# Neighbourhood attention: each head on 32 rows of its own, the scores of two heads issued as a pair

## The chip, the cores and the metric

The program runs on one core of a Trainium2 chip. The time is the device time of one execution in microseconds, the median of the runs shown. TensorE is PE in the profile (PEld are its weight loads), VectorE is DVE, ScalarE is ACT, GpSimd is POOL.

## The reference

Two transformer layers over 64 images of 96 x 96, each cut into 36 patches and a class token (37 tokens of 192 numbers). Layer 0 is a patch embedding, a linear attention with 4 heads of 64 and a soft mixture of 64 experts. Layer 1 is a block with neighbourhood attention and a routed mixture of 8 experts. The change lies in the neighbourhood attention, which sees the 64 x 37 tokens as an image and has 4 heads of 24:

```python
qkv = xs @ qkv_w.T + qkv_b
qkv = qkv.reshape(H, W, 3, nh, dh).transpose(2, 3, 0, 1, 4)
q, kmat, vmat = (qkv[0], qkv[1], qkv[2])
q = q * dh ** (-0.5)
...
logits = jnp.einsum('nhwd,nhawbd->nhwab', q, kk)
...
logits = logits + bias
attn = jax.nn.softmax(logits.reshape(nh, H, W, k * k), axis=-1).reshape(nh, H, W, k, k)
out = jnp.einsum('nhwab,nhawbd->nhwd', attn, vv)
out = out.transpose(1, 2, 0, 3).reshape(H, W, D)
return out @ proj_w.T + proj_b
```

Each query looks at a window of 5 x 5 positions (`k = 5`), clipped at the borders. All is computed in 32-bit floats.

## The kernel before

The 64 rows of 37 tokens are cut into 22 tiles of three rows, 111 tokens each (`TP`). A tile's windows lie in seven rows, so its scores are 111 x 259 (`KW`) per head, with the positions outside the window masked by an added bias.

The stage has two parts. In the first, over pairs of tiles, two small products and a GELU give `xg`, the input in 96 rows by tokens; `keys` multiplies it by `wk` into `kT`. In the second, a pipeline over the tiles, every engine has a list of steps, each with a lag: in turn s a step with lag g works on tile s - g. TensorE's list in each turn is: `query` (lag 0), `values` (3), `scores` of heads 0 and 1 (1), `proj` (5), `scores` of heads 2 and 3 (1), `transpose_w` (3), `fc2` (5), `values_out` (4). VectorE's is: copy of transposed weights (4), `reciprocal` (2), `logits` (1), value copy (3), `spread` (0), `residual` (5). ScalarE does the exponentials (1) and copies, GpSimd multiplies the exponentials by the reciprocal sums (2).

`over_tiles` writes the first 8 turns out straight, then a register loop with four turns per pass, then the last turns straight. In the second part the loop covers turns 8 to 19, on every engine. Engines work strictly in the order of their lists; between them stand semaphores only.

The four heads lie side by side in the 96 rows of `kT`. To keep heads apart, `spread` (L1269) copies the query four times: copy n holds head n's 24 rows and zeros elsewhere (a product with the table `head`). Each of the four score products (L1432) thus contracts over all 96 rows. Heads 0 and 2 write PSUM bank 1, heads 1 and 3 bank 2. A score product waits (`s_nl`) until the head two before it has been emptied from its bank, which is one instruction per head in `logits` (L1296): it adds the bias, writes the scores to SBUF and takes the row maximum. After four heads the maxima are negated (L1298) and ScalarE starts on the exponentials (L1331).

The transposes are L1442 and L1443, the projection L1465, the values in four column strips L1458. In layer 0, L753 is a score product of heads in two halves of 64 rows, in two banks; L738 comes behind it.

## Time and profile before

| | |
|---|---|
| median of 3 runs | 1119.67 us (1112.85 to 1121.09) |
| profiled execution | 1121.94 us, span 1120.0 us |
| TensorE busy | 951.7 us, 85% |
| VectorE busy | 528.6 us, 47% |
| ScalarE busy | 323.8 us, 29% |
| GpSimd busy | 312.6 us, 28% |
| mean granted clock of TensorE | 0.84 |
| first part of the stage | about 580 to 632 us |
| second part of the stage | about 635 to 770 us |

Busy shares are means over stages with different limits. The chain of waits goes back from the last instruction to whatever released it, and so names the engine that sets the pace in each stretch. The timeline lists instructions in order; a bracket behind one says how long its engine was idle before it and who ended that. The end of a product is modelled and includes its way through the array, so records of neighbouring products overlap.

### The profile page before, as it was taken

To read this page: it belongs to the slowest core of one execution; us is meant where nothing else is said; L and a number is where in the kernel's file an instruction comes from. 1 tells how busy PE (TensorE), PEld (TensorE's weight loads), DVE (VectorE), ACT (ScalarE), POOL (GpSimd) and SP (SyncE) were. 2 spreads that over 40 slices of the span, in tenths; PEclk is the share of its full clock that TensorE was granted. 3 is DMA by queue.
4 is the path that set the end of the run, shared out by engine and by line. 5 is a ranking of instruction groups with operands and counts; after the bars stand their busy time and mean duration, and the time that the engine had idled before them with its cause. 6 is when DMAs were issued, how large, how long until landed. Compare 5 with 4: busy or idle time off the path is not lost.

```text
span 1120.0 us, 18357 instructions
## 1 busy us (share of the span) xinstructions
PE 951.7 (85%) x5804; PEld 664.2 (59%) x5804; DVE 528.6 (47%) x1712; ACT 323.8 (29%) x908; POOL 312.6 (28%) x308
## 2 busy tenths in 40 slices
PE   6667999968999998887769899996575999999990
PEld 5555777746664555554545467774563777777670
DVE  5983678864443232222753368864672222222210
ACT  1332233323343322222122256662201222222210
POOL 3881000000000000000042045541017277677444
PEclk9995899975557999999975579996556999999995
DMA  8778000000002999995350000000205244544222
GB/s 253 218 271 346 1 0 0 0 1 1 1 1 80 419 423 422 422 424 215 104 141 1 0 1 2 0 2 8 60 3 140 53 83 82 83 80 74 35 22 21
DMA packets 64187, 125.82 MB, mean 112 GB/s; under 512 B 26910, under 2 KB 47184, under 8 KB 54912
## 3 DMA queue, kind: packets, MB, share of 16 engines
q1 hardware_dynamic: 34176, 115.69, 28.8%
q0 software_dynamic: 29952, 9.36, 6.4%
q8 instruction: 34, 0.56, 0.2%
q14 instruction: 25, 0.20, 0.1%
HBM read 112.83 MB, written 11.98 MB: 111 GB/s over the span
## 4 chain that ended last, share of the span: by engine, by line
PE 67%; DMA 12%; DVE 9%; issue 6%; POOL 2%; ACT 2%; SPq 1%; DVEq 0%; POOLq 0%; ACTq 0%
PE bank L1747 14%; DMA ys<-eo 10%; PE bank L1757 6%; PE bank L738 4%; PE bank L743 3%; PE bank L1432 3%; PE bank L909 2%; PE bank L1518 2%; PE bank L1048 2%; PE bank L927 2%; PE bank L1442 2%; PE bank L1458 2%; PE bank L774 1%; PE bank L907 1%; PE bank L925 1%
## 5 line engine op out<-in xcount | busy, mean ns | idle before, releaser
L1747 PE MATMUL bank<-zT,w 96*128 96x372 f32 x512 | 161.8, 477 | 0.0
L1156 POOL MEMSET xg<- 96x74 f32 x1 | 0.2, 157 | 478.0 <-PE bank L1130 478.0
L1747 PEld LDWEIGHTS bank<-zT,w 96*128 96x128 f32 x512 | 97.4, 191 | 61.0 <-issue 0.5
L1692 POOL DMA_INDIRECT out_dram<-yr,put x48 | 105.7, 2203 | 90.0 <-issue 62.0
L1803 DVE TENSOR_TENSOR hT<-sg,bank 128x372 f32<-128x372 f32 x64 | 34.7, 542 | 126.4 <-PE bank L1747 126.4
L1678 POOL DMA_INDIRECT zr<-z_rows,take x48 | 66.5, 1385 | 85.4 <-issue 83.9
L990 DVE COPY eh<-bank 128x384 f32<-128x384 f32 x32 | 17.8, 558 | 119.4 <-PE bank L1026 119.4
L1048 PE MATMUL bank<-w2s,eg 128*64 128x192 f32 x768 | 69.4, 330 | 0.0
L1776 ACT ACTIVATE sg<-bank 128x372 f32<-128x372 f32 x64 | 30.7, 480 | 128.0 <-PE bank L1747 128.0
L715 PE MATMUL bank<-wtok_g,xT 128*111 128x192 f32 x264 | 47.9, 332 | 20.9 <-DVE y L628 20.9
L1757 PE MATMUL bank<-w2r,hT 128*124 128x192 f32 x384 | 63.7, 326 | 0.0
L1757 PEld LDWEIGHTS bank<-w2r,hT 128*124 128x124 f32 x384 | 62.2, 187 | 0.2
L1022 PE MATMUL bank<-w1s,xy 128*64 128x384 f32 x256 | 49.7, 510 | 12.4 <-DMA w1s<-in_w_dram 11.8
L1048 PEld LDWEIGHTS bank<-w2s,eg 128*64 128x64 f32 x768 | 52.5, 137 | 11.3 <-issue 5.4
L1195 POOL TENSOR_TENSOR nl<-nl,nr 111x1036 f32<-111x1036 f32 x22 | 42.1, 1912 | 61.1 <-DVE nr L1305 61.1
L1331 ACT ACTIVATE nl<-nl,nn 111x259 f32<-111x259 f32 x88 | 43.8, 500 | 48.4 <-DVE nn L1298 48.4
L715 PEld LDWEIGHTS bank<-wtok_g,xT 128*111 128x111 f32 x264 | 41.8, 176 | 26.8 <-DVE y L628 15.3
L1432 PE MATMUL bank<-kT,qx 96*111 (+1 forms) x176 | 53.1, 432 | 1.3 <-DVE nm L1296 1.3
L738 PE MATMUL bank<-hnT,cb 96*128 96x111 f32 x352 | 49.8, 300 | 0.0
L738 PEld LDWEIGHTS bank<-hnT,cb 96*128 96x128 f32 x352 | 45.9, 210 | 2.4 <-issue 0.4
L1296 DVE CUSTOM_DVE_ANT_0 nl<-bank,bias 111x259 f32<-111x259 f32 x88 | 36.7, 424 | 15.2 <-issue 14.7
L743 PE MATMUL bank<-cb,hnT 96*111 96x448 f32 x88 | 41.3, 596 | 0.0
(277 smaller groups left out, 1801.0 us busy)
## 6 DMA issues: line engine op xcount, KB each, us to landing
w1s<-in_w_dram SPq DMA_DIRECT2D x32, 1152.0 KB, 12.6
w2s<-in_w_dram SPq DMA_DIRECT2D x32, 1152.0 KB, 14.7
xt<-in_x_dram SPq DMA_DIRECT2D x22, 336.0 KB, 3.9
xT<-in_xT_dram SPq DMA_DIRECT2D x22, 333.0 KB, 3.6
w<-in_w_dram SPq DMA_DIRECT2D x8, 768.0 KB
ys<-eo SPq DMA_DIRECT2D x64, 48.0 KB, 9.3
w2r<-in_w2r_dram SPq DMA_DIRECT2D x8, 384.0 KB
e<-ys SPq DMA_DIRECT2D x21, 96.0 KB, 2.0
```

The costliest lines, as they stand in the source:

```text
L715: last = nc.tensor.matmul(bank[2 + q % 2][0:TP, 0:ED], xT[q][:, k, :], wtok_g[:, k, :], start=(k == 0), stop=(k == KC - 1))
L738: last = nc.tensor.matmul(bank[1][:, j * TP:(j + 1) * TP], wqk[:, c, j * 128:(j + 1) * 128], hnT[b][:, c, :], start=(c == 0), stop=(c == 1))
L743: last = nc.tensor.matmul(bank[2][0:TP, 0:VGW], hnT[b][:, c, :], wvg[:, c, :], start=(c == 0), stop=(c == 1))
L1022: nc.tensor.matmul(bank[2 * b + part][e * B:(e + 1) * B, 0:HALF_HID], xy[:, 0, p + e * NPAIR, :], w1s[q][:, cols], start=True, stop=False)
L1048: last = nc.tensor.matmul(bank[6 + b][e * B:(e + 1) * B, 0:ED], eg[b][:, j, e, :], w2s[q][:, e, j, :], start=(j == 0), stop=(j == HB - 1))
L1195: nc.gpsimd.tensor_tensor(nl[q][:], nl[q][:], nr[b][:].unsqueeze(2).to_broadcast([TP, NHN, KW]), ALU.mult).then_inc(s_nw, 1)
L1331: last = nc.scalar.activation(nl[q][:, head, :], nl[q][:, head, :], ACT.Exp, bias=nn[b][:, head:head + 1], accum_out=nsum[b][:, head:head ...
L1432: nc.tensor.matmul(bank[1 + head % 2][0:TP, 0:KW], qx[q % 2][:, head, :], kT[:, bass.ds(first, KW)], start=True, stop=True).then_inc(s_nS, 1)
L1678: nc.gpsimd.indirect_dma_start(zr[b][:, j, :], None, z_rows, bass.IndirectOffsetOnAxis(ap=take[:, k:k + 1], axis=0), bounds_check=NROW - 1 ...
L1692: nc.gpsimd.indirect_dma_start(rows_out, bass.IndirectOffsetOnAxis(ap=put[:, k:k + 1], axis=0), yr[e % 2][:, j, :], None, bounds_check=OUT ...
L1747: last = nc.tensor.matmul(bank[2 + 2 * (m % 2) + part][:, 0:HS], w13[b][:, c, at:at + 128], zT[b][:, c, half * HS:(half + 1) * HS], start= ...
L1757: last = nc.tensor.matmul(bank[6 + j % 2][0:SP_, 0:ED], hT[:, m, j * SP_:(j + 1) * SP_], w2r[b][:, m, :], start=(m == 0), stop=(m == EH // ...
```

## The change

Weights and biases of queries and keys are padded from 96 to 128 columns, so that head n lies in rows 32n to 32n + 23 and zeros follow. `qx` is then one copy of 128 x 111 instead of 96 x 4 x 111, made by a plain add-and-scale. A score product takes its head's 32 rows of `qx` and `kT`. The waits on `s_nl` move ahead of each pair: heads 0 and 1 wait until all four heads of the tile before have been emptied, heads 2 and 3 until heads 0 and 1 have. Ahead of the queries of tiles 0, 1 and 2, six products of `identity` with 256 columns of `kT` are added, whose result nobody reads. TensorE's list is written out straight for all turns (`straight`); the other engines keep their loops.

```diff
--- before.py
+++ after.py
@@ -60,10 +60,10 @@
 PACK_B = [("wqk", HALF, 2 * QKW), ("wvg", HALF, 2 * VGW), ("wo", 128, 2 * ED), ("causal", TP, 2 * TP),
           ("phi", HALF, 2 * NE), ("scale", HALF, 1), ("image", TP, GB + 1), ("b1s", 128, NE * HB)]
 
-PACK_C = [("fc1", HALF, 2 * WN), ("conva", WN, CONV), ("convb", CONV, WN), ("wq", WN, WN), ("wk", WN, WN),
+PACK_C = [("fc1", HALF, 2 * WN), ("conva", WN, CONV), ("convb", CONV, WN), ("wq", WN, 128), ("wk", WN, 128),
           ("wv", WN, WN), ("proj", NHN * VW, WN), ("fc2", WN, ED), ("bv", TP, WN), ("bfc2", TP, ED),
-          ("bfc1", WN, 1), ("bconva", CONV, 1), ("bconvb", WN, 1), ("bq", WN, 1), ("bk", WN, 1), ("bproj", WN, 1),
-          ("head", WN, NHN), ("router", HALF, 2 * EX), ("before", TP, TP), ("count", TP, SP_), ("number", TP, T), ("spare", SP_, NST), ("real", TP, T),
+          ("bfc1", WN, 1), ("bconva", CONV, 1), ("bconvb", WN, 1), ("bq", 128, 1), ("bk", 128, 1), ("bproj", WN, 1),
+          ("router", HALF, 2 * EX), ("before", TP, TP), ("count", TP, SP_), ("number", TP, T), ("spare", SP_, NST), ("real", TP, T),
           ("gain", HALF, 2 * EX)]
 
 
@@ -101,6 +101,13 @@
                 step(i + (u - lag), (u - lag) % unroll)
     for s in range(stop, n + lags):
         turn(s)
+
+
+def straight(stages, n, buffers):
+    for s in range(n + max(lag for lag, _ in stages)):
+        for lag, step in stages:
+            if 0 <= s - lag < n:
+                step(s - lag, (s - lag) % buffers)
 
 
 def tower(nc, ins, rows_out):
@@ -261,7 +268,7 @@
         near = [sb(f"near{v}", [TR, NHN, KW]) for v in range(2)]
         bias = [sb(f"bias{v}", [TP, NHN, KW]) for v in range(4)]
         xg = sb("xg", [WN, XCOLS])
-        kT = sb("kT", [WN, XCOLS])
+        kT = sb("kT", [128, XCOLS])
         hp = [sb(f"hp{b}", [TP, 2, ED]) for b in range(2)]
         hpT = [sb(f"hpT{b}", [HALF, 2, PAIR]) for b in range(2)]
         fx = [sb(f"fx{b}", [WN, PAIR]) for b in range(2)]
@@ -270,7 +277,7 @@
         vsrc = [sb(f"vsrc{b}", [WN, TP]) for b in range(2)]
         vn = [sb(f"vn{q}", [TP, NHN, VW]) for q in range(4)]
         vl = [sb(f"vl{i}", [TP, NHN, VW]) for i in range(3)]
-        qx = [sb(f"qx{b}", [WN, NHN, TP]) for b in range(2)]
+        qx = [sb(f"qx{b}", [128, TP]) for b in range(2)]
         nl = [sb(f"nl{q}", [TP, NHN, KW]) for q in range(4)]
         nm = [sb(f"nm{b}", [TP, NHN]) for b in range(2)]
         nn = [sb(f"nn{b}", [TP, NHN]) for b in range(2)]
@@ -1254,7 +1261,7 @@
 
             def keys(p, b):
                 dve.wait_ge(s_fK, p + 1)
-                nc.vector.tensor_scalar(kT[:, bass.ds(PADR * S + p * PAIR, PAIR)], bank[4][0:WN, 0:PAIR], Cc["bk"], None, ALU.add).then_inc(s_fKc, 1)
+                nc.vector.tensor_scalar(kT[:, bass.ds(PADR * S + p * PAIR, PAIR)], bank[4][:, 0:PAIR], Cc["bk"], None, ALU.add).then_inc(s_fKc, 1)
 
             over_tiles(dve, [(0, normalize), (4, convb), (2, fc1), (5, keys)], T // 2)
 
@@ -1266,7 +1273,7 @@
                     dve.wait_ge(s_fV, t)
                 if after(t, 2):
                     dve.wait_ge(s_nS, 4 * t - 4)
-                nc.vector.scalar_tensor_tensor(out=qx[b][:], in0=bank[0][0:WN, 0:TP].unsqueeze(1).to_broadcast([WN, NHN, TP]), scalar=Cc["bq"], in1=Cc["head"].unsqueeze(2).to_broadcast([WN, NHN, TP]), op0=ALU.add, op1=ALU.mult).then_inc(s_nq, 1)
+                nc.vector.tensor_scalar(qx[b][:], bank[0][:, 0:TP], Cc["bq"], float(np.float32(DN ** -0.5)), ALU.add, ALU.mult).then_inc(s_nq, 1)
 
             def value(j, dst):
                 dve.wait_ge(s_fV, j + 1)
@@ -1392,20 +1399,23 @@
                 pe.wait_ge(s_fg, p + 1)
                 if after(p, 1):
                     pe.wait_ge(s_fKc, p)
-                nc.tensor.matmul(bank[4][0:WN, 0:PAIR], Cc["wk"], xg[:, bass.ds(PADR * S + p * PAIR, PAIR)], start=True, stop=True).then_inc(s_fK, 1)
+                nc.tensor.matmul(bank[4][:, 0:PAIR], Cc["wk"], xg[:, bass.ds(PADR * S + p * PAIR, PAIR)], start=True, stop=True).then_inc(s_fK, 1)
 
             over_tiles(pe, [(3, convb), (0, transpose_h), (1, fc1), (2, conva), (4, keys)], T // 2)
             pe.wait_ge(s_fKc, T // 2)
             pe.wait_ge(s_hTc, 2 * T + T // 2)
 
             def query(t, q):
+                if isinstance(t, int) and t < 3:
+                    for _ in range(6):
+                        nc.tensor.matmul(bank[5][:, 0:256], ident, kT[:, 0:256], start=True, stop=True)
                 if after(t, 1):
                     pe.wait_ge(s_nq, t)
                 if after(t, 4):
                     pe.wait_ge(s_fVc, t - 1)
                 elif t == 0:
                     pe.wait_ge(s_fVc, 2)
-                nc.tensor.matmul(bank[0][0:WN, 0:TP], Cc["wq"], xg[:, bass.ds(PADR * S + t * TP, TP)], start=True, stop=True).then_inc(s_nQ, 1)
+                nc.tensor.matmul(bank[0][:, 0:TP], Cc["wq"], xg[:, bass.ds(PADR * S + t * TP, TP)], start=True, stop=True).then_inc(s_nQ, 1)
 
             def value(j, b):
                 pe.wait_ge(s_fv, j + 1)
@@ -1424,12 +1434,13 @@
                 value(j, j)
 
             def scores(t, q, heads):
-                first = (B - WIN + PADR) * S if isinstance(t, int) and t == T - 1 else t * TP
+                first = (B - WIN + PADR) * S if t == T - 1 else t * TP
                 pe.wait_ge(s_nq, t + 1)
+                if t or heads[0]:
+                    pe.wait_ge(s_nl, 4 * t + heads[0])
                 for head in heads:
-                    if after(t, 1) or head >= 2:
-                        pe.wait_ge(s_nl, 4 * t + head - 1)
-                    nc.tensor.matmul(bank[1 + head % 2][0:TP, 0:KW], qx[q % 2][:, head, :], kT[:, bass.ds(first, KW)], start=True, stop=True).then_inc(s_nS, 1)
+                    rows = slice(head * VW, (head + 1) * VW)
+                    nc.tensor.matmul(bank[1 + head % 2][0:TP, 0:KW], qx[q % 2][rows, :], kT[rows, first:first + KW], start=True, stop=True).then_inc(s_nS, 1)
 
             def transpose_w(t, q):
                 pe.wait_ge(s_nw, t + 1)
@@ -1468,8 +1479,8 @@
                 pe.wait_ge(s_nz, t + 1)
                 nc.tensor.matmul(bank[7][0:TP, 0:ED], nz[q % 2][:], Cc["fc2"], start=True, stop=True).then_inc(s_nF, 1)
 
-            over_tiles(pe, [(0, query), (3, values), (1, lambda t, q: scores(t, q, (0, 1))), (5, proj),
-                            (1, lambda t, q: scores(t, q, (2, 3))), (3, transpose_w), (5, fc2), (4, values_out)], T, unroll=4, tail=2)
+            straight([(0, query), (3, values), (1, lambda t, q: scores(t, q, (0, 1))), (5, proj),
+                      (1, lambda t, q: scores(t, q, (2, 3))), (3, transpose_w), (5, fc2), (4, values_out)], T, 4)
 
 
         def route_act(act):
@@ -1922,14 +1933,14 @@
             for n in range(NHN):
                 near[v // 2, 0:TP, n] = np.where(ok, rpb[n][np.where(ok, dr, 0), np.where(ok, dt, 0)], 0)
     qkv, bqkv = f["L1_attn_qkv_w"], f["L1_attn_qkv_b"]
+    heads = lambda a: np.pad(a.reshape(-1, NHN, DN), ((0, 0), (0, 0), (0, VW - DN))).reshape(-1, NHN * VW)
     cc = pack_rows(PACK_C, {
         "fc1": chunks(f["L1_attn_fc1_w"].T), "conva": f["L1_attn_convA_w"].T, "convb": f["L1_attn_convB_w"].T,
-        "wq": qkv[0:WN].T, "wk": qkv[WN:2 * WN].T, "wv": qkv[2 * WN:].T, 
+        "wq": heads(qkv[0:WN].T), "wk": heads(qkv[WN:2 * WN].T), "wv": qkv[2 * WN:].T, 
         "proj": np.pad(f["L1_attn_proj_w"].T.reshape(NHN, DN, WN), ((0, 0), (0, VW - DN), (0, 0))).reshape(NHN * VW, WN),
         "fc2": f["L1_attn_fc2_w"].T, "bv": rows(bqkv[2 * WN:], TP), "bfc2": rows(f["L1_attn_fc2_b"], TP),
         "bfc1": col(f["L1_attn_fc1_b"]), "bconva": col(f["L1_attn_convA_b"]), "bconvb": col(f["L1_attn_convB_b"]),
-        "bq": col(bqkv[0:WN]), "bk": col(bqkv[WN:2 * WN]), "bproj": col(f["L1_attn_proj_b"]),
-        "head": (np.arange(WN)[:, None] // DN == np.arange(NHN)[None, :]).astype(np.float32) * np.float32(DN ** -0.5),
+        "bq": heads(bqkv[None, 0:WN]).T, "bk": heads(bqkv[None, WN:2 * WN]).T, "bproj": col(f["L1_attn_proj_b"]),
         "router": chunks(f["L1_ffn_gate_w"].T), "before": (w[:, None] < w[None, :]).astype(np.float32),
         "count": np.tile(np.arange(SP_, dtype=np.float32)[None, :], (TP, 1)),
         "spare": 1.0 + B * S + np.arange(SP_)[:, None] + SP_ * (np.arange(NST) % SJ)[None, :],
```

TensorE, the first turns of the second part, before (L1414 value, L1408 query, L1432 scores):

```order
L1414 MATMUL bank<-cc,vsrc 111x96 x2
L1408 MATMUL bank<-xg,cc 96x111 x2
L1432 MATMUL bank<-kT,qx 111x259 x4
L1408 MATMUL bank<-xg,cc 96x111
L1432 MATMUL bank<-kT,qx 111x259 x4
L1408 MATMUL bank<-xg,cc 96x111
```

and the same place in the changed kernel (L1424 value, L1411 the added products, L1418 query, L1443 scores):

```order
L1424 MATMUL bank<-cc,vsrc 111x96 x2
L1411 MATMUL bank<-kT,identity 128x256 x6
L1418 MATMUL bank<-xg,cc 128x111
L1411 MATMUL bank<-kT,identity 128x256 x6
L1418 MATMUL bank<-xg,cc 128x111
L1443 MATMUL bank<-kT,qx 111x259 x4
L1411 MATMUL bank<-kT,identity 128x256 x6
L1418 MATMUL bank<-xg,cc 128x111
```

The order of queries and scores is the same; six wide products stand ahead of each of the first three queries.

TensorE, the start of a loop pass, before:

```order
L98 UNCONDITIONAL_BRANCH
L1405 REGISTER_ALU
L1408 ISA
L1408 MATMUL bank<-xg,cc 96x111
L1414 MATMUL bank<-cc,vsrc 111x96
L1431 ISA
L1432 ISA
L1432 MATMUL bank<-kT,qx 111x259 x2
L1462 REGISTER_ALU
L1464 REGISTER_ALU
L1465 MATMUL bank<-noT,cc 96x111
```

and the same turn in the changed kernel:

```order
L1418 MATMUL bank<-xg,cc 128x111
L1424 MATMUL bank<-cc,vsrc 111x96
L1443 MATMUL bank<-kT,qx 111x259 x2
L1476 MATMUL bank<-noT,cc 96x111
L1443 MATMUL bank<-kT,qx 111x259 x2
```

The products stand in the same order, with the projection between the two pairs of scores; the register and branch instructions are gone.

## Rows read from the trace of the kernel before

**Rows 1.** The page: busy time, share and instructions of each engine.

```profile
PE 951.7 (85%) x5804; PEld 664.2 (59%) x5804; DVE 528.6 (47%) x1712; ACT 323.8 (29%) x908; POOL 312.6 (28%) x308
```

**Rows 2.** Stretches: length, busy (count) of PE, PEld, DVE, ACT, POOL; PEclk, DMA, GB/s.

```profile
580.00:635.00 55.00, 52.35 (x135) 26.03 (x135) 19.21 (x49) 14.44 (x31) 13.06 (x13) 0.50 0.01 4
635.00:656.00 21.00, 17.59 (x53) 11.93 (x54) 9.38 (x48) 7.08 (x26) 4.91 (x5) 0.50 0.00 0
656.00:757.00 101.00, 97.53 (x1021) 75.45 (x1019) 77.51 (x359) 65.43 (x231) 51.21 (x59) 1.00 0.01 1
757.00:857.00 100.00, 57.07 (x314) 50.86 (x315) 59.59 (x191) 14.91 (x39) 20.02 (x17) 0.52 0.21 53
```

**Rows 3.** Chain of waits, 628 to 775: start us, us, what was waited for.

```profile
634.95 0.70 PE bank L1408 x2
...
655.21 0.88 PE bank L1432 x2
...
666.95 1.10 PE bank L1432 x4
...
672.16 1.10 PE bank L1432 x4
...
677.22 1.03 PE bank L1432 x4
...
691.10 0.89 PE bank L1432 x4
692.18 1.03 PE bank L1432 x4
...
732.31 1.03 PE bank L1432 x4
...
746.47 0.47 PE bank L1432 x2
```

**Rows 4.** Timeline of a loop turn: start us, us, engine, line, operation [idle before].

```profile
690.94 1.05 PE L1432 MATMUL bank<-kT,qx 96*111 x4
...
691.60 0.42 DVE L1296 CUSTOM_DVE_ANT_0 nl<-bank,bias 111x259 f32<-111x259 f32 x1 [0.19 <-issue]
...
692.39 0.08 DVE L1296 DVE_READ_ACCUMULATOR2_ANT nm<- 111x1 f32 x1
692.52 0.27 PEld L1432 LDWEIGHTS bank<-kT,qx 96*111 96x111 f32 x2 [0.17 <-DVE nm L1296]
692.82 0.42 DVE L1296 CUSTOM_DVE_ANT_0 nl<-bank,bias 111x259 f32<-111x259 f32 x1 [0.35 <-issue]
...
693.05 0.36 PE L1442 MATMUL bank<-identity,nl 111*111 111x111 f32 x2
...
694.63 0.35 PEld L1458 LDWEIGHTS bank<-pTa,vn 111*32 111x32 f32 x16 [0.24 <-issue]
...
695.92 0.19 ACT L1331 ACTIVATION_READ_ACCUMULATOR nl<-nl,nn 111x1 f32 x1
...
696.47 0.17 DVE L1305 RECIPROCAL nr<-nsum 111x4 f32<-111x4 f32 x1
...
696.59 0.42 DVE L1296 CUSTOM_DVE_ANT_0 nl<-bank,bias 111x259 f32<-111x259 f32 x1
```

**Rows 5.** Timeline of a turn that is written out straight.

```profile
666.72 0.08 DVE L1296 DVE_READ_ACCUMULATOR2_ANT nm<- 111x1 f32 x1
...
666.95 1.10 PE L1432 MATMUL bank<-kT,qx 96*111 96x259 f32 x4 [0.16 <-DVE nm L1296]
```

**Rows 6.** Timeline of layer 0's attention, scores of heads in 64 rows.

```profile
155.80 0.65 PE L753 MATMUL bank<-qk 64*111 64x111 f32 x8
...
156.38 0.81 PE L738 MATMUL bank<-hnT,cb 96*128 96x111 f32 x5
```

**Rows 7.** Timeline, the first query copy.

```profile
635.67 0.68 DVE L1269 SCALAR_TENSOR_TENSOR qx<-bank,cc 96x444 f32<-96x444 f32 x1 [0.78 <-PE bank L1408]
```

**Rows 8.** TensorE by stretch, first routed expert: length, busy (count), PEclk, DMA, GB/s.

```profile
857.00:858.00 1.00, 1.00 (x4) 0.84 0.28 55
```

## The prediction

> **What bounds the kernel now.** I began with the engine table of the page: TensorE is busy for 85% of the span [rows 1]. Such a share is an average over stages, so the next view is the table of stretches [rows 2]. The change touches three of them: the projections before attention (580 to 635), the first turns of attention (635 to 656) and its steady part (656 to 757). In the first two TensorE ran at half clock (0.50), in the third at full clock. In the third it was busy for 97.5 of 101 us, VectorE for 77.5, ScalarE for 65.4, GpSimd for 51.2. The reader is to see there that the steady part looks like a TensorE limit with VectorE not far behind.
>
> The chain of waits [rows 3] confirms it and gives the beat. One turn handles one tile. From 677.22 to 732.31 lie 11 turns of the register loop: 5.01 us each. A turn written out straight takes 5.21 (666.95 to 672.16). The 18 turns from tile 3 (655.21) to tile 21 (746.47) take 91.3 us. Two scores of 259 columns take 0.89, so one takes 0.44; 692.18 less the end of the four records at 691.99 leaves 0.19 for the projection of 111 columns.
>
> The timeline of a loop turn [rows 4] shows the order that matters: first scores at 690.94, first transpose at 693.05, which is 2.11 us for four scores (1.78) and the projection, with almost nothing idle. VectorE empties head 0 from 691.60, that is 0.22 after its columns have streamed (690.94 + 0.44), and is through with head 1 at 692.47: 0.87 for two heads. TensorE reacts to that within 0.05 (692.52). This eviction now lies beside TensorE's own work, because head 1 streams while head 0 is emptied.
>
> There is a second ring, nearly as long: evictions from 691.60, negated maxima, ScalarE's exponentials until 696.11 (695.92 + 0.19), reciprocal, next eviction at 696.59. That is 4.99 us with only some 0.26 of slack (696.11 to 696.59, less 0.17 for the reciprocal and 0.05 to react).
>
> **The change, part by part.**
>
> *Scores in pairs.* Do two heads on different rows run together at all? Nothing in the attention of the second layer shows it, but the first layer does: four products of 64 rows and 111 columns, in two row halves and two banks, take 0.58 us until the next group starts [rows 6]. One after the other they would be 4 x 0.19 = 0.76. In pairs they are 0.38, and the remaining 0.20 is what going in and out of the split array costs. So a pair of scores should take 0.44 in place of 0.89, and TensorE's streaming falls by 2 x 0.44 = 0.89 us per tile.
>
> That 0.20 is the first bill. Today the turn changes the shape of the array three times (into the values in column strips, to their 37-row part, back). The change adds four: into the scores, out to the projection, into the scores, out to the transposes. If each were exposed, 0.80 of the 0.89 would be gone again. The Trainium skill's page "TensorEngine Tiling (Array Packing)", Key Properties, says that changing the tiling mode, unlike changing the tile, drains the TensorE; by that rule the gain on TensorE alone is 0.09 per turn, and the rows agree with a drain: 0.20 as worked out, and 0.24 in which no weights load ahead of the value strips [rows 4].
>
> *The wait.* This is the larger bill. Before, head 2 waited for head 0 alone, head 3 for head 1. Now both heads of the second pair wait until both of the first have been emptied, and both of the first land at the same moment. Between the pairs TensorE has only the projection (0.19, with a switch on each side still under the 1.14 of waiting). I rebuild the piece from the end of the value product to the first transpose:
> switch in 0.20; pair 0.44; until VectorE starts 0.22; two evictions 0.87; reaction 0.05; weights of the second pair, taken as half a switch, 0.10; pair 0.44; switch out 0.20. Sum 2.52, against 2.11 before: **+0.41 per loop turn**, so 5.40.
> The other ring: from the end of head 1's eviction to the start of head 2's went 0.35 (692.47 to 692.82 in [rows 4]); now 0.05 + 0.10 + 0.44 + 0.22 = 0.81, so +0.46, less the 0.26 of slack: 5.19. The first ring is the longer one; the second is the floor: +0.20.
> In straight turns the reactions are slower: eviction done at 666.80, scores again at 666.95 [rows 5]. That already makes them 5.21; they pay some 0.36 more.
> Steady part: 12 x 0.41 + 6 x 0.36 = **+7.1**. Floor 18 x 0.20 = +3.6. If all four switches were exposed beside the wait (two more of 0.20, no cover by the projection), 18 x 0.6 = +11 is the ceiling.
>
> *Queries without the four-fold copy.* VectorE's 0.68 per tile [rows 7] becomes an eviction of 111 columns in place of 444. It lies in VectorE's time behind the evictions and a whole turn ahead of its reader, in the steady part. Worth nothing there; should VectorE's spare time vanish it would be worth up to 0.4. In the first turns it lies on the path and is counted below.
>
> *Warming products.* 18 products of 128 rows and 256 columns stand ahead of the first three queries. By the score row, six take 2.6 at full clock, 5.2 at half. Before: first query at 634.95, scores of tile 3 at 655.21 [rows 3], all at half clock [rows 2]. In the expert stage at the end it rose soon after dense wide products began: half clock on the mean to 857 [rows 2], 0.84 in the stretch 857 to 858 [rows 8]; I take it that the first batch does the same. Then: batch one 634.6 to 638.9 (four slow, two fast); query; batch two to 641.8; scores of tile 0 to 644.6; batch three to 647.2; scores of tile 1 to 650.1; evictions, maxima and query copy 1.4; query, value and scores of tile 2 to 654.4; transposes 1.2; again a query copy, scores of tile 3 at 656.5. **+1.3** us. Bounds: -2 if the clock is up after the first two products, +5 if only in the second batch.
>
> *Straight code on TensorE.* Register and branch instructions go; a loop border costs 0.1 (three of them). I count nothing; the straight turns in front show no gap between them, which speaks against code loading as a cost.
>
> *Keys and queries with 128 columns of weights.* Eleven loads a third longer than about 0.1 us, at half clock: +0.4, bounds 0 and 1.
>
> **Sum:** 7.1 + 1.3 + 0.4 = +8.8. The profiled execution took 1121.9 (span 1120.0 and 1.9 around it), which gives 1130.7. It lies 2.3 above the median 1119.7; I add the sum to the median: **1128.5**.
>
> **The rivals.**
>
> A. *TensorE's freed time wins (faster).* If the first pair is out by the time the projection has streamed, and switches are hidden, the turn falls to 4.99 - 0.89 + 2 x 0.20 = 4.50, capped by the second ring. With a ring as before that is no gain; for a gain both evictions have to take under about 0.5 us in place of 0.87, or the second ring has to shrink as well. The price is 4.50 less 4.99 = -0.49 in each of 22 tiles, -11, and -2 at the start: 1107. Against it stand the eviction rows [rows 4]. Chance 0.07. The Trainium skill's page "TensorEngine Tiling (Array Packing)", Theoretical Speedup, promises up to 4x for a contraction of at most 32 and is the reason why one would expect this.
>
> B. *The clock stays up into routing (faster).* The 100 us from 757 to 857 ran at 0.52 with TensorE 57 us busy [rows 2]. If a shifted tail kept it up, up to half of that goes: near 1100. The tail's chain is not touched. Chance 0.04.
>
> C. *Heads do not overlap in 32-row strips.* The pair takes 0.89. The first pair's second half hides under head 0's eviction, the second does not: 18 x 0.44 = +8 more, 1136. Speaks against it: [rows 6], though those are 64-row halves. Chance 0.07.
>
> D. *The clock does not rise, or falls back.* Half-array products might not hold it, and 580 to 635 shows narrow products, busy 95%, that never raised it [rows 2]. A turn streams 4.99 - 0.89 - 3 x 0.20 = 3.5 us; at half clock that comes a second time: 18 x 3.5 = +63, and +5 at the start: 1188. It needs the warming products to fail; once up, the clock held through the first layer's pairs. Chance 0.07.
>
> The forecast (a new wait between the pairs, covered only in part) has 0.75; its own range is 1121 (floor, +1) to 1137 (ceiling, +17).
>
> **How the numbers follow.** Range: the own range, stretched to C above and towards A and the scatter of the three runs (1112.9 to 1121.1) below: 1115 to 1140. Out of it lie D, B and most of A. What this kernel can tell from no change is about 1%, 11 us: faster means below 1108.5, slower above 1130.9. The forecast's centre is 2.4 below that upper line, so of its 0.75 some 0.45 falls within and 0.29 above, 0.01 below. C adds 0.06 above and 0.01 within, D 0.07 above, A 0.05 below and 0.02 within, B 0.02 and 0.02: faster 0.08, same 0.50, slower 0.42.
>
> **What would show it.** A turn of 5.3 to 5.5 in the chain, with a VectorE eviction in it in every turn, not TensorE alone; VectorE's first two evictions back to back right behind a pair, and TensorE idle for 0.5 to 1 us before the second pair; pairs that start within hundredths of each other; granted clock 1.0 from about 638. Wrong: a turn under 5.0 (then the evictions were not the wait), clock at 0.5 past 645 (D), or pairs as long as two scores (C). Most fragile is the 0.20 per switch, read from halves and not from quarters.

## The result and the profile after

The changed kernel takes 1183.07 us (median of 4 runs, 1180.96 to 1185.9) against 1119.33 for the kernel before. The ratio is 1.0582 (95% interval 1.0534 to 1.0631): slower by 64 us. The forecast was 1128.5, with 1140 as its upper end. Rival D, the clock that falls back, had been priced at 1188 and given a chance of 0.07; that is what came. Medians below are of all executions, ratios leave out those that lie more than 1.5% above the fastest of the same kernel.

The engine table of the page, and its line of TensorE's granted clock in 40 slices of 29.6 us (tenths of full speed):

```profile
PE 1008.2 (85%) x5840; PEld 695.3 (59%) x5840; DVE 516.4 (44%) x1712; ACT 326.2 (28%) x908; POOL 312.6 (26%) x308
...
PEclk9995999955559999999657566655555999999996
```

TensorE is busy 56.5 us longer than in [rows 1] with nearly the same number of instructions, and its share is 85% both times: the share hides the loss. VectorE's work fell by 12. The second line shows where to look: from the twentieth slice (562 us) on, through the whole neighbourhood attention, the digits are 5 to 7.

The same stretches as [rows 2], up to the end of attention (columns: length, busy and count of PE, PEld, DVE, ACT, POOL; PEclk, DMA, GB/s):

```profile
580.00:635.00 55.00, 52.85 (x136) 27.29 (x135) 18.74 (x47) 14.44 (x31) 12.85 (x13) 0.50 0.01 4
635.00:656.00 21.00, 16.21 (x74) 11.74 (x73) 6.07 (x42) 4.17 (x16) 4.26 (x4) 0.83 0.00 0
656.00:757.00 101.00, 93.99 (x640) 64.15 (x639) 44.27 (x238) 45.07 (x154) 32.45 (x36) 0.60 0.00 1
757.00:825.00 68.00, 59.37 (x399) 40.69 (x400) 25.96 (x134) 25.88 (x88) 22.01 (x27) 0.56 0.00 1
```

Up to 635 nothing moved. In the first turns the clock is higher than before (0.83 in place of 0.50), which is the warming products at work. In the steady part it is 0.60 where it was 1.00, and in the same 101 us TensorE gets through 640 instructions in place of 1021, although it is busy for 94 of them. That busy time cannot be set beside the 97.5 of [rows 2] as it stands: the same product lasts nearly twice as long at half clock. Where the clock was up for most of a stretch (700 to 704, 0.93), TensorE was busy for 3.39 of 4 us. Attention goes on past 800.

Around the place where the clock falls, in stretches of 1 or 2 us (same columns):

```profile
638.00:639.00 1.00, 1.00 (x5) 0.86 (x4) 0.00 (x0) 0.00 (x0) 0.00 (x0) 0.71 0.00 0
...
650.00:652.00 2.00, 0.81 (x6) 0.71 (x8) 1.10 (x7) 1.07 (x5) 0.15 (x1) 1.00 0.00 0
652.00:653.00 1.00, 0.58 (x4) 0.05 (x2) 0.00 (x0) 1.00 (x5) 0.00 (x0) 0.62 0.00 0
653.00:654.00 1.00, 0.00 (x0) 0.00 (x0) 0.94 (x7) 0.01 (x1) 0.70 (x1) 0.50 0.00 0
```

The clock rose within the first batch (0.71 in 638 to 639), as forecast. It fell in 652 to 653, when TensorE had been idle for more than half of the time since 650. That could still be an episode. What costs the time is that it did not come back for good. In the chain of waits (start us, us, what) of the steady part:

```profile
702.50 0.69 PE bank L1443 x4
...
709.48 0.69 PE bank L1443 x4
...
731.93 1.20 PE bank L1443 x4
...
740.86 1.20 PE bank L1443 x4
...
749.78 1.20 PE bank L1443 x4
```

L1443 x4 is a pair of scores (two records per head). It lasts 0.69 at full clock and 1.20 at half. A turn takes 8.93 when all of it runs at half clock (731.93 to 740.86, 740.86 to 749.78) and 6.98 when the clock comes up for a part of it (702.50 to 709.48); it was 5.01 before [rows 3].

One piece at full clock shows what the change itself does (the first and the last row are from elsewhere, the first scores of tiles 3 and 21; timeline: start us, us, engine, line, operation [idle before]):

```profile
658.54 1.21 PE L1443 MATMUL bank<-kT,qx 32*111 32x259 f32 x4
...
700.83 0.27 PEld L1443 LDWEIGHTS bank<-kT,qx 32*111 32x111 f32 x4
700.84 0.69 PE L1443 MATMUL bank<-kT,qx 32*111 32x259 f32 x4
...
701.57 0.42 DVE L1303 CUSTOM_DVE_ANT_0 nl<-bank,bias 111x259 f32<-111x259 f32 x1 [0.88 <-issue]
...
702.27 0.08 DVE L1303 DVE_READ_ACCUMULATOR2_ANT nm<- 111x1 f32 x1
702.47 0.30 PEld L1443 LDWEIGHTS bank<-kT,qx 32*111 32x111 f32 x4 [0.77 <-issue]
702.50 0.69 PE L1443 MATMUL bank<-kT,qx 32*111 32x259 f32 x4 [0.61 <-DVE nm L1303]
703.12 0.45 PE L1453 MATMUL bank<-identity,nl 111*111 111x111 f32 x2
...
703.55 0.58 PE L1453 MATMUL bank<-identity,nl 111*111 111x111 f32 x2
...
804.59 1.21 PE L1443 MATMUL bank<-kT,qx 32*111 32x259 f32 x4
```

Four records (two heads) take 0.69 where one head alone would stream for 0.44: the heads do run together. VectorE empties both back to back, TensorE waits 0.61 behind the projection, and from the first pair to the first transpose go 2.28 (700.84 to 703.12) against 2.11 in [rows 4]. The row at 703.55 (two transposes in 0.58 where [rows 4] has 0.36) is the clock falling again.

The 64.0 us by place, on the profiled spans (1184.0 and 1120.0): the scores of tile 3 start at 658.54, before at 655.21, +3.3. From there to the scores of tile 21 (804.59) go 146.1 in place of 91.3, +54.8. Behind them 379.4 in place of 373.5, +5.9, of which the last turns of attention are a part. (The starts before are from the chain, the later ones from the timeline; the two views differ by up to 0.2.)

### The profile page after: what moved, and what is told of

It is laid out like the page before. It is cut to its first block, busy times and chain, and to the rows that moved or that the text cites. A ratio compares the mean times of both kernels' runs of the same rounds, so it can differ in the third digit from the quotient of the medians.

```text
span 1184.0 us, 18365 instructions
## 1 busy us (share of the span) xinstructions
PE 1008.2 (85%) x5840; PEld 695.3 (59%) x5840; DVE 516.4 (44%) x1712; ACT 326.2 (28%) x908; POOL 312.6 (26%) x308
## 4 chain that ended last, share of the span: by engine, by line
PE 65%; DMA 11%; DVE 10%; issue 8%; POOL 2%; ACT 2%; SPq 1%; DVEq 0%; POOLq 0%; ACTq 0%
PE bank L1758 14%; DMA ys<-eo 9%; PE bank L1768 5%; PE bank L745 4%; PE bank L1453 3%; PE bank L750 3%; PE bank L1443 2%; PE bank L916 2%; PE bank L1529 2%; PE bank L1055 2%; PE bank L934 2%; PE bank L781 1%; PE bank L1454 1%; PE bank L932 1%; PE bank L914 1%
## 5 line engine op out<-in xcount | busy, mean ns | idle before, releaser
L1758 PEld LDWEIGHTS bank<-zT,w 96*128 96x128 f32 x512 | 97.8, 192 | 61.4 <-issue 1.1
L1443 PE MATMUL bank<-kT,qx 32*111 32x259 f32 x176 | 42.9, 571 | 14.0 <-DVE nm L1303 14.0
L1303 DVE CUSTOM_DVE_ANT_0 nl<-bank,bias 111x259 f32<-111x259 f32 x88 | 34.3, 423 | 44.8 <-issue 44.8
L1453 PE MATMUL bank<-identity,nl 111*111 111x111 f32 x176 | 52.1, 407 | 0.2 <-issue 0.2
L1453 PEld LDWEIGHTS bank<-identity,nl 111*111 111x111 f32 x176 | 42.4, 302 | 12.1 <-issue 10.3
```

Source lines behind the costliest of these rows:

```text
L1443: nc.tensor.matmul(bank[1 + head % 2][0:TP, 0:KW], qx[q % 2][rows, :], kT[rows, first:first + KW], start=True, stop=True).then_inc(s_nS, 1)
L1453: nc.tensor.transpose(bank[3 + head // 2][0:TP, k:k + TP], nl[q][:, head, c * TP:(c + 1) * TP], ident[0:TP, 0:TP])
L1758: last = nc.tensor.matmul(bank[2 + 2 * (m % 2) + part][:, 0:HS], w13[b][:, c, at:at + 128], zT[b][:, c, half * HS:(half + 1) * HS], start= ...
```

## The experiments

Two theories stood at the start. **Rows**: a score product now fills 32 rows of the array in place of 96, two at a time, and such work does not hold the clock, however busy TensorE is. **Idle**: the new wait (0.61 us per turn) lets the clock fall. Both would give the same trace of the changed kernel. The clock and TensorE's busy time below are those of 656 to 757, in one profiled execution each. For e5 to e8 there is a second profiled execution of the same kernel: it has a clock of 0.69 (e5), 0.55 (e6), 0.53 (e7) and 0.98 (e8), so that a single figure is good to about 0.1 where the clock goes up and down. As above, busy times are comparable only between rows with about the same clock.

| kernel | median us | ratio to before (95%) | clock | busy of 101 | loop turn, us |
|---|---|---|---|---|---|
| before | 1119.3 to 1121.2 | 1 | 1.00 | 97.5 | 4.99 to 5.01 |
| changed | 1183.07 | 1.058 (1.053 to 1.063) | 0.60 | 94.0 | 8.93 at half clock |
| e1 wide filler | 1141.16 | none: two of four left out | 0.96 | 97.4 | 5.38 |
| e2 wait alone | 1130.89 | 1.010 (1.006 to 1.014) | 1.00 | 93.1 | 5.42 |
| e3 warming alone | 1122.66 | 1.002 (0.998 to 1.006) | 0.95 | 94.3 | |
| e4 no warming | 1179.69 | 1.052 (1.047 to 1.057) | 0.57 | 95.2 | |
| e5 waits per head | 1170.17 | 1.044 (1.038 to 1.051) | 0.62 | 98.0 | 8.83 at half clock |
| e6 narrow filler | 1185.16 | 1.058 (1.053 to 1.063) | 0.64 | 100.4 | |
| e7 second pair moved | 1196.43 | 1.067 (1.063 to 1.071) | 0.53 | 94.3 | 8.7 at half clock |
| e8 filler, longer start | 1130.96 | 1.009 (1.006 to 1.012) | 1.00 | 96.1 | 5.39 |
| e9 halves, moved | 1193.63 | 1.067 (1.064 to 1.070) | 0.60 | 89.4 | |
| e10 halves | 1134.41 | 1.012 (1.009 to 1.016) | 0.98 | 88.3 | 5.39 |
| e11 e9 without warming | 1183.27 | 1.058 (1.054 to 1.061) | 0.90 (in the fastest, 1167.49) | 78.5 | 6.56 to 6.73 |
| e12 e9 with cover | 1191.00 | 1.063 (1.059 to 1.067) | 0.60 | 89.7 | |
| e13 e12 without warming | 1182.77 | 1.057 (1.052 to 1.062) | 0.64 | 89.5 | |

**One wide product more per turn.** It stands behind the projection, into a part of a bank that nobody reads.

```diff
+            def fill(t, q):
+                nc.tensor.matmul(bank[0][:, 256:512], ident, kT[:, 0:256], start=True, stop=True)
...
-            straight([..., (5, proj),
+            straight([..., (5, proj), (1, fill),
```

> The changed kernel with one more product of 128 rows and 256 columns in every turn, between the first and the second pair of scores, where TensorE waits for VectorE (its result is not read). Theory 1 (the clock: the pairs and the wait leave TensorE too little dense work to keep its full clock, and nearly all of the 64 us come from that): the granted clock stays at 1.00 from 640 to the end of the stage, a turn takes 5.3 to 5.6 us instead of 7.0 to 8.9, and the kernel about 1128 us, +8 to +12 on before. Rival (the wait and the array switches cost the time themselves, the low clock being only a companion): the turns stay above 6.5 us and the kernel above 1150, whatever the clock.

Stretch of the steady part and two beats of the chain:

```profile
656.00:757.00 101.00, 97.40 (x973) 64.22 (x971) 65.17 (x342) 61.26 (x218) 47.73 (x53) 0.96 0.01 2
```

```profile
693.37 0.69 PE bank L1443 x4
...
698.75 0.69 PE bank L1443 x4
```

The four runs lie at 1132.2, 1132.7, 1149.6 and 1152.7; the two longer ones had a lower mean clock (0.83 and 0.825 against 0.846), so part of the attention stayed cold in them. In the profiled one the clock is 0.50 from 650 to 663 and 1.00 from 664 on. The turn is then 5.38: adding work to TensorE, inside its wait, takes some 3.5 us out of every turn that ran at half clock. The turn came as expected; the clock from 640 on and the 1128 did not. The result fits both theories, since the product fills rows and fills idle time.

**The wait without the narrow rows.** The kernel before, with the change's waits alone: its scores stay on 96 rows.

```diff
+                if after(t, 1) or heads[0]:
+                    pe.wait_ge(s_nl, 4 * t + heads[0])
                 for head in heads:
-                    if after(t, 1) or head >= 2:
-                        pe.wait_ge(s_nl, 4 * t + head - 1)
```

> The kernel before, with one thing of the change alone: both heads of the second pair wait until both heads of the first have been emptied, and likewise between tiles. Products keep 96 rows and run one after the other. Theory 1a (idle time alone brings the clock down): clock at 0.5 for long stretches, the kernel at 1160 or more. Theory 1b (idle time and half-empty array together are needed): clock stays at 1.00; the first pair takes 0.89, head 0 is emptied beside head 1, so the turn grows by about 0.22 + 0.44 + 0.05 + 0.10 - 0.19 = 0.6 us, the kernel by 13 us to 1132.

Stretch, then chain, then timeline:

```profile
656.00:757.00 101.00, 93.14 (x947) 72.64 (x946) 73.91 (x349) 63.64 (x224) 49.27 (x54) 1.00 0.00 1
```

```profile
680.35 1.13 PE bank L1432 x4
...
685.78 1.13 PE bank L1432 x4
```

```profile
690.28 0.42 DVE L1296 CUSTOM_DVE_ANT_0 nl<-bank,bias 111x259 f32<-111x259 f32 x1
...
691.06 0.08 DVE L1296 DVE_READ_ACCUMULATOR2_ANT nm<- 111x1 f32 x1
...
691.20 1.13 PE L1432 MATMUL bank<-kT,qx 96*111 x4 [0.34 <-DVE nm L1296]
```

TensorE now idles in every turn (busy for 93.1 of 101 us, before 97.5), and the clock stays at 1.00. That is evidence against the idle theory, but not yet the end of it: these waits are shorter than those of the changed kernel (0.34 against 0.61 ahead of the second pair), which at full clock was busy for only 3.39 of 4 us. The run with heads on 64 rows, below, has the full wait. The wait alone costs 11 us (5.42 per turn in place of 4.99 to 5.01). Head 0's eviction still starts while head 1 streams (690.28, 0.66 behind the pair's start at 689.62), so pairing of the streams saves the turn almost nothing: 5.42 with four scores one after the other, 5.38 to 5.39 with pairs.

**The warming products alone**, in the kernel before (its identity has 96 rows there), and **the change without them**.

```diff
+                if isinstance(t, int) and t < 3:
+                    for _ in range(6):
+                        nc.tensor.matmul(bank[5][:, 0:256], identity[0:WN, :], kT[:, 0:256], start=True, stop=True)
```

> The kernel before with the 18 warming products of the change alone (96 rows of them instead of 128, since kT has 96). Both theories: the clock is at 1.00 from 638 and, with four full score products per turn, stays there. The first score of tile 3 then comes near 655 as before (batches of 2.6 us against the halved turns), so the kernel lies within 3 us of before. If the clock falls again behind the third batch, as in the changed kernel, it must recover by itself within a few turns and the cost is up to 10 us.

```diff
-                if isinstance(t, int) and t < 3:
-                    for _ in range(6):
-                        nc.tensor.matmul(bank[5][:, 0:256], ident, kT[:, 0:256], start=True, stop=True)
```

> The changed kernel without the 18 warming products. Theory 1 with the warming as useless (the clock fell at 652 in the changed kernel anyway): about 1180 us, within 5 of the changed kernel's 1183. If the warming had helped at least in part, the clock stays at 0.50 throughout and the kernel takes 1190 to 1205.

Alone they change nothing that can be measured (1.0019, 0.998 to 1.0058), and without them the change takes 1179.69, 3 less than with them. The clock in the steady part is 0.57 without and 0.60 with them. They neither cause nor prevent the loss. (The 0.95 of the kernel before with them is no fall within attention: the clock is 1.00 from 636 to 744, and attention ends earlier in this execution, the fastest but one of ten.)

**The change with the old waits**, so that each head waits for the one two before it.

```diff
-                if t or heads[0]:
-                    pe.wait_ge(s_nl, 4 * t + heads[0])
                 for head in heads:
+                    if t or head >= 2:
+                        pe.wait_ge(s_nl, 4 * t + head - 1)
```

> The changed kernel with the old waits: each score product waits only for the head two before it. Products keep 32 rows, so the first pair still runs together, the second starts head by head. Theory 1b' (what brings the clock down is that the array is filled to half or less during scores, with or without the wait): clock near 0.55 in 656 to 757 and a time within 8 us of the changed kernel's 1183. Rival (the wait is needed as well): clock at 1.00 from about 660, a turn of about 5.1 to 5.3, kernel at 1122 to 1135.

Stretch and chain:

```profile
656.00:757.00 101.00, 97.95 (x656) 68.54 (x654) 45.19 (x244) 46.77 (x161) 34.29 (x38) 0.62 0.00 1
```

```profile
692.14 0.95 PE bank L1443 x3
...
699.02 0.95 PE bank L1443 x3
```

TensorE is busy for 98.0 of 101 us at a clock of 0.62. The turns of the rows above, in which the clock is up for a part, take 6.88 (6.98 in the changed kernel), and those at half clock 8.83 (8.93). Taking the wait away gives back 13 us of 64 and leaves the clock low; the time lies between the two that were expected, 5 us outside the nearer one. The second profiled execution (clock 0.69) shows how much idle time is left when the clock is up: TensorE busy for 3.74 of 4 us in 732 to 736, at 0.93, and the clock still falls behind it. Beside the pairwise waits on 96 rows this is the crossed pair: waits with wide rows (3.66 of 4 us busy at full clock, 684 to 688), 1.00; shorter ones with narrow rows, 0.62 to 0.69.

**The same filler on 32 rows.**

```diff
-                nc.tensor.matmul(bank[0][:, 256:512], ident, kT[:, 0:256], start=True, stop=True)
+                nc.tensor.matmul(bank[0][:, 256:512], identity[0:VW, :], kT[0:VW, 0:256], start=True, stop=True)
```

> As the kernel with one filling product per turn, but the filling product contracts over 32 rows instead of 128; it streams the same 256 columns, so TensorE's busy time per turn is the same. Theory A (the clock follows how long TensorE streams): clock and time as with the wide filling product, turns of 5.4, 1132 to 1150. Theory B (it follows how much of the array works): clock low as in the changed kernel, 1170 to 1185.

Stretch of this kernel, its filler in the timeline, and the filler of the wide version:

```profile
656.00:757.00 101.00, 100.43 (x684) 69.78 (x684) 46.43 (x251) 46.37 (x159) 34.28 (x38) 0.64 0.01 1
```

```profile
705.53 0.69 PE L1483 MATMUL bank<-kT,identity 32*128 32x256 f32 x2
```

```profile
703.37 0.61 PE L1483 MATMUL bank<-kT,identity 128*128 128x256 f32 x2
```

Place, number of columns and count are the same; only the rows differ. TensorE is now busy for 100.43 of 101 us and the clock is 0.64, against 0.96 with 128 rows. This is the cleanest row of the study: a TensorE without any gap at half clock for most of the time. In the second profiled execution one sees both that the clock does not rise over 26 us without a gap, and that it falls without one (same columns):

```profile
664.00:690.00 26.00, 26.00 (x158) 17.57 (x158) 10.03 (x55) 9.93 (x35) 8.03 (x9) 0.50 0.00 1
694.00:695.00 1.00, 1.00 (x6) 0.51 (x6) 0.46 (x5) 0.35 (x1) 1.00 (x2) 1.00 0.00 0
...
696.00:697.00 1.00, 1.00 (x7) 1.00 (x7) 0.77 (x5) 0.59 (x3) 0.00 (x0) 0.50 0.00 0
```
 The Trainium skill's page "TensorE: Matmul & The Clock Gate", section "HAM oscillation — how this bites in real kernels", puts a clock that falls back down to stretches in which the engine idles; this run differs from it (a fall between 695 and 696 with TensorE busy throughout), and the measurement decides.

**The wide filler with a longer start**: a fourth batch of warming products, ahead of tile 3.

```diff
-                if isinstance(t, int) and t < 3:
-                    for _ in range(6):
-                        nc.tensor.matmul(bank[5][:, 0:256], ident, kT[:, 0:256], start=True, stop=True)
+                if isinstance(t, int) and t < 4:
+                    for _ in range(6 if t < 3 else 4):
+                        nc.tensor.matmul(bank[4 if t == 3 else 5][:, 0:256], ident, kT[:, 0:256], start=True, stop=True)
```

> As the kernel with a wide filling product per turn, with four more warming products ahead of the fourth query, where TensorE waited 1.3 us and the clock fell at 651. Theory 1: the clock stays at 1.00 from 640 to 768, the 12 us at half clock from 651 to 663 are gone (some 4 us), and the runs no longer scatter to 1150: about 1128, +8 on before. If the clock falls somewhere else, 1132 to 1150 as before.

Stretch and timeline:

```profile
656.00:757.00 101.00, 96.06 (x985) 63.47 (x982) 66.54 (x350) 63.74 (x226) 49.36 (x54) 1.00 0.01 2
```

```profile
656.93 0.69 PE L1443 MATMUL bank<-kT,qx 32*111 32x259 f32 x4
...
662.53 0.69 PE L1443 MATMUL bank<-kT,qx 32*111 32x259 f32 x4
...
668.08 0.69 PE L1443 MATMUL bank<-kT,qx 32*111 32x259 f32 x4
...
754.73 0.69 PE L1443 MATMUL bank<-kT,qx 32*111 32x259 f32 x4
```

Now nothing falls (in the second profiled execution it falls once, near 660, and is back at 664), and the kernel takes 1130.96, or 1.0091 (1.0059 to 1.0122) of before. This comes close to the forecast's kernel with its assumed clock, though not quite: it carries a filling product in every turn, inside the wait, and four more warming products. Set beside the forecast: tile 3's scores at 656.93 (forecast 656.5), 97.8 us for the 18 turns (before 91.3, so +6.5; forecast +7.1), straight turns of 5.55 (forecast 5.57), loop turns of 5.39 (forecast 5.40).

**Heads on 64 rows.** The query is copied twice (each copy masked to every other head), and a pair takes heads 0 and 2, then 1 and 3, on the two halves of the array. All else is as in the change.

```diff
-                nc.vector.tensor_scalar(qx[b][:], bank[0][:, 0:TP], Cc["bq"], float(np.float32(DN ** -0.5)), ALU.add, ALU.mult).then_inc(s_nq, 1)
+                for i in range(2):
+                    last = nc.vector.tensor_scalar(qx[b][:, i, :], bank[0][:, 0:TP], Cc["bq"], Cc["half"][:, i:i + 1], ALU.add, ALU.mult)
+                last.then_inc(s_nq, 1)
...
-                for head in heads:
-                    rows = slice(head * VW, (head + 1) * VW)
-                    nc.tensor.matmul(bank[1 + head % 2][0:TP, 0:KW], qx[q % 2][rows, :], kT[rows, first:first + KW], start=True, stop=True).then_inc(s_nS, 1)
+                for k in heads:
+                    rows = slice(64 * (k % 2), 64 * (k % 2) + 64)
+                    nc.tensor.matmul(bank[1 + k % 2][0:TP, 0:KW], qx[q % 2][rows, k // 2, :], kT[rows, first:first + KW], start=True, stop=True).then_inc(s_nS, 1)
```

> The changed kernel with one thing altered: pairs of 64-row halves instead of 32-row strips, as in the run beside it, in the changed kernel's own order (second pair right behind the wait). Theory B: clock at 1.00 in the steady part, turns of 5.4, so about 1128 to 1135. Theory B' or rival (the waits bring it down whatever the rows): clock low, 1170 to 1185.

Stretch and timeline:

```profile
656.00:757.00 101.00, 88.28 (x948) 60.69 (x946) 71.95 (x369) 62.18 (x221) 47.66 (x53) 0.98 0.01 2
```

```profile
703.11 0.69 PE L1446 MATMUL bank<-kT,qx 64*111 64x259 f32 x4
...
704.77 0.69 PE L1446 MATMUL bank<-kT,qx 64*111 64x259 f32 x4 [0.61 <-DVE nm L1306]
...
708.50 0.69 PE L1446 MATMUL bank<-kT,qx 64*111 64x259 f32 x4
```

A pair takes 0.69 as on 32 rows, and the wait ahead of the second is the same 0.61. At full clock TensorE is busy for 3.39 of 4 us (704 to 708), just as the changed kernel was where its clock was up, and for 88.3 of the 101 us, yet the clock is 0.98. This settles the idle theory for the waits of the change: the same idle time on 64 rows keeps the clock. Here, too, the clock falls between 652 and 653, but it is back at 659 and stays; in the changed kernel it was still at 0.50 at 676. The kernel takes 1134.41, with one more query copy of 0.33 on VectorE than the change. So 1183.07 less 1134.41, **49 of the 64 us, hang on 32 against 64 rows** under the same waits.

**The second pair behind the transposes.** Three attempts to hide the wait by other work of TensorE, none of which helped. The first has the change's rows; VectorE's list is split so that the reciprocal stands between the two pairs of evictions.

```diff
-            straight([(0, query), (3, values), (1, lambda t, q: scores(t, q, (0, 1))), (5, proj),
-                      (1, lambda t, q: scores(t, q, (2, 3))), (3, transpose_w), (5, fc2), (4, values_out)], T, 4)
+            straight([(0, query), (3, values), (1, lambda t, q: scores(t, q, (0, 1))), (5, proj), (3, transpose_w),
+                      (5, fc2), (1, lambda t, q: scores(t, q, (2, 3))), (4, values_out)], T, 4)
```

> The changed kernel with the second pair of scores moved behind the transposes and the second projection in TensorE's list, so that the wait for two evictions is covered by 1.9 us of other products; on VectorE the reciprocal stands between the two pairs of evictions, so that the second ring does not grow. At full clock the turn is 4.99 - 0.89 + 3 x 0.20 = 4.7 us, and the kernel 18 x 0.3 = 5 us faster than before, 1115. Theory A (streaming time decides the clock): TensorE never idles, clock 1.00, about 1115. Theory B (filled rows decide it): clock low in part, 1150 to 1180, with turns of 8 us and more where it is low.

1196.43, clock 0.53, outside the expected 1150 to 1180. A turn takes some 8.7 in place of 8.93 at half clock: the cover is worth 0.2 of a cold turn, and more turns were cold.

The second has this order and the 64-row halves, the third (a pair with and without the warming products, as the second is) also lets VectorE make values and query copy ahead of its second pair of evictions (its list, abbreviated, against that of the change):

```diff
-(4, copy_w), (2, reciprocal), (1, logits), (3, values), (0, spread), (5, residual)
+(4, copy_w), (1, logits 0 1), (2, reciprocal), (3, values), (0, spread), (1, logits 2 3), (5, residual)
```

> Heads on 32 rows as in the changed kernel, but each score product contracts over a half of 64 rows: the query is copied twice, once with heads 1 and 3 zero and once with heads 0 and 2 zero, and a pair is made of heads 0 and 2, then 1 and 3, in rows 0 to 63 and 64 to 127. A pair still streams 259 columns once, but now fills all 128 rows. The second pair stands behind the transposes and the second projection, the reciprocal between the two pairs of evictions. Theory B (the clock follows how many rows of the array work, zeros or not): clock at 1.00 from some turn near 655 to the end of the stage, turns of 4.7 to 4.8 us, and some 5 us faster than before: 1113 to 1118. Theory B' (zeros do not count, only useful data): clock low as with the 32-row products, 1180 to 1200.

> As the kernel with halves and the moved pair, without the 18 warming products. If the dense turns raise the clock by themselves as in the kernel before (at 656), the time is within 3 us of the run with warming products; if not, 1180 or more.

> As the kernel with 64-row halves and the second pair behind the transposes, with VectorE's value copy and query copy moved ahead of the second pair of evictions. In the run before it, TensorE waited up to 1.2 us per turn for the query copy, which stood behind evictions that now come late. Theory B: with that wait gone the turn is 4.7 to 4.9 us at full clock, clock 1.00, and the kernel 1113 to 1118. If the turn again shows the low clock, what holds it is more than the filled rows of the scores, and the time is 1170 or more.

> The same without the 18 warming products: within 3 us of its sibling if the turns raise the clock by themselves, 1170 or more if not.

They take 1193.63 and 1183.27, 1191.00 and 1182.77 (each with and without the warming products). The 1113 to 1118 that were expected of rows filled with zeros did not come; "1170 or more" did. The stretch of the second (the third has 89.72 and 0.60 as well):

```profile
656.00:757.00 101.00, 89.37 (x618) 60.51 (x615) 45.57 (x238) 40.69 (x144) 30.64 (x34) 0.60 0.00 1
```

and from the waits of each (who <- for whom: us, times, longest), 656 to 800:

```profile
PEld bank L1423 <- DVE qx L1277: 19.7, 17, 1.4
```

```profile
PEld bank L1481 <- ACT noT L1359: 19.2, 16, 1.8
```

In the second TensorE now waits for the query copy, 17 times, in the third for ScalarE's `noT`, 16 times: the wait had only moved. The clock is 0.60 in both, with 64-row halves. So 64 rows are not sufficient by themselves.

The second version without the warming products shows what this order costs when the clock is up. Its profiled execution is the fastest of six (1167.49; the others took 1179 to 1191), with a clock of 0.90. Stretch, then timeline:

```profile
656.00:757.00 101.00, 78.51 (x749) 52.91 (x749) 54.14 (x286) 48.59 (x174) 38.94 (x43) 0.90 0.01 1
```

```profile
675.08 0.69 PE L1445 MATMUL bank<-kT,qx 64*111 64x259 f32 x4
...
677.79 0.47 PE L1420 MATMUL bank<-xg,cc 96*128 96x111 f32 x2 [1.18 <-DVE qx L1277]
...
681.81 0.69 PE L1445 MATMUL bank<-kT,qx 64*111 64x259 f32 x4
```

From one second pair to the next go 6.73 us at full clock (675.08 to 681.81, the clock at 1.00 throughout), and 6.56 in the loop, where 4.7 to 4.9 had been expected and the order of the change takes 5.39. TensorE is busy for only 10.31 of the 14 us from 675 to 689, less than in any version that kept its clock. In the same turn the evictions of the second pair start at 675.98 only, the four exponentials run from 677.00 to 679.00 behind them, and behind these comes the copy `noT` (679.00) that the projection needs: the moved pair lengthens the other ring. So this order loses by itself even at full clock, and it idles more. Whether that idle time is what pulls the clock down there, with 64 rows, no run separates.

## Why the prediction failed

**The failed step is the clock.** Every duration in the sum was read at full clock, and the forecast took for granted that the steady part would stay at 1.00. The prediction wrote of D: "It needs the warming products to fail; once up, the clock held through the first layer's pairs." The first half is wrong: the warming products worked (0.71 in 638 to 639, then 1.00 to 652) and the clock fell all the same, and in the kernel without them the outcome is the same. The second half was a false likeness: the pairs of the first layer fill 64 rows (clock 1.00 from 120 to 236), and 64 rows hold the clock here too, in the change's own order (0.98 against 0.60). The row that spoke for D was in the prediction: 580 to 635, TensorE busy 95% at 0.50 [rows 2]. It had shown that busy time alone does not raise the clock, and it should have weighed more than 0.07. The word "narrow" fits it badly, though: its products contract over 64 to 111 rows, with 64 to 111 columns of weights.

**D's price per turn was right, its total in part by luck.** It priced 3.5 us per turn at half clock, beside the turn of 5.40. Measured: 8.93 less 5.38 to 5.40 is 3.5. Over the 18 turns the clock cost less than D's 63: of the 54.8, 6.5 are there at full clock too, which leaves 48.3, because the clock rose for parts of some turns (6.98). D's sum had left out the +7.1 of the wait, and the two errors offset each other in part: 1188 against 1183.

**The pairs do overlap** (rival C wrong): 0.69 for the four records, the next load 0.62 behind the pair's start, where 0.44 + 0.20 had been taken.

**The wait was right, in place and size.** The piece, step by step at full clock: VectorE starts 0.73 behind the first pair (taken 0.66), its two evictions and the reaction end in a second pair at 702.50, 1.66 behind the first, and the first transpose follows 0.62 later. That is 2.28; the prediction's sum for the same piece, without the switch ahead of it, is 2.32. Against the 2.11 of [rows 4] the piece alone gives 0.17 of the turn's 0.4; the rest lies elsewhere in the turn, where the prediction had its switch in; no row shown here places it. With the clock held, all beats came within 0.04 us of the forecast. The whole is +10.5 us (1130.96 against 1120.46) for a sum of 8.8; the profiled executions put +1.7 ahead of tile 3, +6.5 in the 18 turns and +1.0 behind them. The wait alone, without strips, padding or warming products, cost 11. Rival A falls with it: TensorE's freed streaming is spent waiting for evictions. The Trainium skill's page "TensorEngine Tiling (Array Packing)", section "PSUM Bottleneck", says that tiling speeds up the TensorE and not the emptying of PSUM; the trace agrees, with two evictions back to back of 0.35 to 0.42 each in every turn.

**The query copy** takes 0.33 in place of 0.68 [rows 7], and at full clock no beat shows a gain from it, as forecast. **The start** is 0.4 later than forecast in the version that keeps its clock (656.93, with four more warming products), and 2.0 in the changed kernel (658.54), since there the clock fell at 652, ahead of tile 3. **Straight code and padded weights**: no row shows a cost.

What is shown: with waits, order and counts equal, the rows that the products fill decided here whether the clock came back (32 against 128 rows in one product per turn; 32 against 64 rows in the scores). That the idle wait of the change is not the cause is shown by the same wait on 64 rows (0.98) and by the TensorE without gaps (0.64). It is no general rule that wide rows bring the clock up: before the change TensorE was busy for 40 of the 40 us from 588 to 628, on 64 to 111 rows, at 0.50 throughout. Rows and rows times columns of weights were not told apart; every pair of runs here that differs in one differs in the other. What stays open besides: what pulls the clock down in the other order on 64 rows, and why the same kernel with the wide filler regains the clock earlier in some executions than in others. No version ran faster than the kernel before; the best with narrow scores is 1.009 of it.

## What to carry to other kernels

Before you split the array to save streaming, ask of every row that you use as a price at which clock it was taken, and whether the new work keeps that clock: look for a stretch of the same kernel with products as narrow as the new ones, and read its granted clock beside its busy time; where there is none, the clock is an assumption that wants a chance of its own. TensorE's busy share says nothing of it, since it was 85% before and after: at half clock the same work counts as more busy time. And when two producers land together in place of one after the other, write down who empties them: the time saved in streaming turns into a wait for the evictions unless the consumer was idle.

## What the runs showed of the hardware

- A TensorE busy for 100.4 of 101 us ran at a mean granted clock of 0.64, with its scores and one more product per turn on 32 rows of the array; one busy for 88.3 with 64-row halves ran at 0.98. With that one product of 256 columns on 128 rows instead of 32 the 0.64 became 0.96.
- A clock lost to a gap comes back or not according to the work behind it: it was at 0.50 from 653 to 659 in the 64-row version and from 650 to 663 in the one with the wide filler, and both then stayed at 1.00 to 764; in the changed kernel it rose only for pieces of single turns.
- The clock also fell without any gap: with the filler on 32 rows TensorE was busy throughout 692 to 700, at 1.00 in 694 to 695 and at 0.50 in 696 to 697; and it stayed at 0.50 over 26 us without a gap (664 to 690). Before the change it did so over 40 us (588 to 628), with products on 64 to 111 rows.
- Two products of 259 columns on two 32-row strips, in two banks, take 0.69 from first start to last end, as on two 64-row halves. From such a pair to the next load with another shape go 0.62, of which some 0.2 is beyond the streaming.
